# A state-space block with attention and routed experts on one core: three input blocks per half, the residual added on TensorE, ones brought in by transfers

## The reference

```python
x_in, z = split(x @ W_in)                         # 512 + 512 features
x_in = silu(sum(x_pad[:, k:k+L] * W_conv[k] for k in range(4)) + b_conv)
dbc = x_in @ W_xproj                              # 64 + 16 (B) + 16 (C)
dt = softplus(dbc[..., :64] @ W_dt + b_dt)
def step(state, inp):                             # state [batch, 512, 16], 512 steps one after another
    dA = exp(clip(dt_t[:, :, None] * A, -10, 10))
    state = clip(state * dA + x_t[:, :, None] * (dt_t[:, :, None] * B_t[:, None, :]), -10, 10)
    y_t = einsum('bdn,bn->bd', state, C_t) + D * x_t
y = y * silu(z)
out = y @ W_out                                   # added to what the attention and expert branch gives
```

## Time and profile before

| | |
|---|---|
| three runs | 4441.67 us median, 4422.38 to 4448.53 |
| profiled execution, own time | 4426.43 us |
| its span | 4424.3 us |
| busy: PE, PEld | 3743.7 us (85%), 2801.6 us (63%) |
| busy: DVE, ACT, POOL | 2973.9 us (67%), 2502.9 us (57%), 2202.6 us (50%) |
| state-space part | from 2175.6 us to the end |

### The profile page before, as it was taken

The page is one execution under the profiler, slowest core; times in us unless marked ns, Lnnn a source line. Parts: engine busy times, 40 slices in busy tenths (PEclk is TensorE's granted clock), DMA queues, the critical chain, the costliest instruction groups (busy, mean ns, idle before and its releaser), DMA issues.

```text
span 4424.3 us, 70363 instructions
## 1 busy us (share of the span) xinstructions
PE 3743.7 (85%) x22136; PEld 2801.6 (63%) x22136; DVE 2973.9 (67%) x5485; ACT 2502.9 (57%) x6473; POOL 2202.6 (50%) x1120
## 2 busy tenths in 40 slices
PE   4888888888888875999869888889898998988886
PEld 2344444444444434777658888878787887888776
DVE  4455455544545522222269999999999999999997
ACT  1443343434433431333378777788778787777773
POOL 2223333333333221000067777777777787777774
PEclk8899999999999987999989999999999999999998
DMA  3322232223322214666522222222222222222221
GB/s 91 95 77 83 84 100 79 78 88 98 91 87 80 79 54 128 212 209 211 150 87 92 76 87 78 80 88 86 78 89 87 75 92 76 87 81 77 87 82 36
DMA packets 285737, 419.86 MB, mean 95 GB/s; under 512 B 77397, under 2 KB 249814, under 8 KB 262808
## 3 DMA queue, kind: packets, MB, share of 16 engines
q1 hardware_dynamic: 273048, 381.12, 26.6%
q0 software_dynamic: 12288, 33.57, 2.2%
HBM read 330.63 MB, written 83.17 MB: 94 GB/s over the span
## 4 chain that ended last, share of the span: by engine, by line
POOL 22%; issue 10%; PE 9%; DVE 8%; ACT 1%; DVEq 0%; POOLq 0%; DMA 0%; SPq 0%; ACTq 0%
POOL m_ub L1530 18%; PE m_Y L1884 7%; DVE m_PR L1734 2%; DVE m_S L1742 2%; DVE m_PR L1742 2%; DVE m_S L1734 1%; POOL m_th_z L1515 1%; POOL m_yg L1540 1%; DVE m_ub L1719 1%; ACT m_dA L1640 1%; POOL m_dtx L1509 1%; PE m_F L1846 1%; PE m_F L1895 0%; PE m_F L1820 0%; DVEq L1733 0%
## 5 line engine op out<-in xcount | busy, mean ns | idle before, releaser
L1530 POOL TENSOR_TENSOR m_ub<-m_Bb,m_dtx 128x2048 f32<-128x2048 f32 x256 | 1157.7, 4546 | 440.4 <-PE m_Y L1884 434.0
L1640 ACT ACTIVATE m_dA<-m_dt,m_a_neg 128x128 f32<-128x128 f32 x4096 | 1211.0, 387 | 168.8 <-DVE m_S L1742 167.6
L1884 PE MATMUL m_Y<-m_ub,m_ident 128*128 128x128 f32 x8192 | 1040.4, 293 | 204.6 <-DVE m_ub L1719 204.6
L1884 PEld LDWEIGHTS m_Y<-m_ub,m_ident 128*128 128x128 f32 x8192 | 1022.1, 208 | 218.4 <-DVE m_ub L1719 218.4
L539 ACT ACTIVATE f_pt<-f_X 128x512 f32<-128x512 f32 (+1 forms) x704 | 371.8, 554 | 712.9 <-PE f_X L841 691.2
L615 DVE TENSOR_REDUCE f_nm<-f_Y 128x1 f32<-128x512 f32 (+3 forms) x896 | 434.1, 530 | 354.4 <-PE f_Y L841 351.4
L1734 DVE SCALAR_TENSOR_TENSOR m_PR<-m_dA,m_S 128x512 f32<-128x512 f32 x512 | 355.6, 695 | 124.5 <-POOL m_ub L1530 53.8
L1734 DVE SCALAR_TENSOR_TENSOR m_S<-m_dA,m_PR 128x512 f32<-128x512 f32 x512 | 354.9, 693 | 12.0
L1742 DVE CUSTOM_DVE_ANT_1 m_PR<-m_PR,m_ub 128x512 f32<-128x512 f32 x512 | 353.2, 690 | 0.2 <-DVE m_PR L1734 0.2
L1742 DVE CUSTOM_DVE_ANT_1 m_S<-m_S,m_ub 128x512 f32<-128x512 f32 x512 | 353.2, 690 | 0.0
L1719 DVE TENSOR_TENSOR m_ub<-m_S,m_Cb 128x512 f32<-128x512 f32 x512 | 349.7, 683 | 0.0
(11 more groups left out here) (229 smaller groups left out, 6278.4 us busy)
## 6 DMA issues: line engine op xcount, KB each, us to landing
m_Bb<-m_bc_dram SPq DMA_DIRECT2D x64, 1024.0 KB, 4.6
m_Cb<-m_bc_dram SPq DMA_DIRECT2D x64, 1024.0 KB, 4.7
f_parts_dram<-f_parts SPq DMA_DIRECT2D x32, 768.0 KB, 4.1
f_kst<-f_parts_dram SPq DMA_DIRECT2D x192, 128.0 KB, 2.6
f_qst<-f_parts_dram SPq DMA_DIRECT2D x192, 128.0 KB, 2.6
e_rows<-sorted_rows SPq DMA_DIRECT2D x70, 256.0 KB, 2.7
e_wg<-Wg SPq DMA_DIRECT2D x70, 256.0 KB, 2.9
e_wu<-Wu SPq DMA_DIRECT2D x70, 256.0 KB, 3.9
```

The source lines that it names most:

```text
L1530: pool.tensor_tensor(ub[:, h, i, :, :], Bb[:, s, :, :], dtx[:, par, m, None, s * SN:(s + 1) * SN].to_broadcast([P, NST, SN]), ALU.mult).th ...
L1640: last = act.activation(dA[:, h, i, n, :], dtt[:, par, m, s * SN:(s + 1) * SN], ACT.Exp, scale=a_neg[:, m, n:n + 1])
L1884: last = pe.matmul(Y[:, i * SN:(i + 1) * SN], ident[:, :], ub[:, h, i, n, :], start=False, stop=(n == NST - 1), skip_group_check=True)
```

## The change

In the state-space part `ub` gets a third block per half. Inputs go to blocks 0 and 1; `times_c` writes to blocks 1 and 2, and `nsum` reads those. So the inputs of block 0 need only the end of the scan of unit u-2, and those of block 1 only the first half of its `nsum`. Room for it comes from tiles that now share storage: `xn` is `xm`, `sp_u` is `th_z`, `sp_v` is `th_x`, `ot` is `res`, and `dtx` is single. Waits go with that: the load of rows waits for the transposes, the load of `res` for the store of the chunk before, and the two tanh of ScalarE for the dt of the chunk before. `add_res` goes away: TensorE adds `res` with two more matmuls of 128x256 at the end of `project_out`, and ScalarE copies F[2] out (`copy_out`). For the very first unit, dt, dt times x and the inputs are made on VectorE instead of GpSimd.

In the attention part the two memsets of ones go away; ScalarE issues six transfers of one partition each from a tile of ones, and the waits of ScalarE and TensorE for all weights move to "T" and "lat" of the first sequence.

```diff
-        fixed(pool.memset(onesb)) among the later constants      # now among the first seven
-        act.wait_ge(w_loaded, W_ALL)
+        act.wait_ge(const_ready, N_CONST_FIRST)
+        for p in range(2):
+            for q in range(PARTS):
+                act.dma_start(kst[p][KS + q:KS + q + 1, :, :]..., onesb[:, 0:NH * SEQ // P]).then_inc(q_scaled, 16)
...
-        for p in range(2):
-            dve.memset(kst[p][KS:KS + PARTS, :, :], 1.0).then_inc(q_scaled, 1)
...
-    xn = sb("m_xn", [P, TT, DM])
+    xn = xm
-    sp_u = sb("m_sp_u", [P, MI, CN])
-    sp_v = sb("m_sp_v", [P, MI, CN])
+    sp_u = th_z
+    sp_v = th_x
-    dtx = sb("m_dtx", [P, 2, MI, CN])
+    dtx = sb("m_dtx", [P, MI, CN])
-    ub = sb("m_ub", [P, 2, 2, NST, SN])
+    ub = sb("m_ub", [P, 2, 3, NST, SN])
-    ot = sb("m_ot", [P, TT, DM])
+    ot = res
...
         def load_res(c):
-            held(ot_done, c)
+            held(ot_stored, 16 * c)
...
         def inputs_of(c, par, u):
-                    pool.wait_ge(nsum_done[pu], 2 * (pc - 1) + i + 1)
+                    if i == 0:
+                        pool.wait_ge(s_step, NU * ST * (pc - 1) + ST * (pu + 1) + 2)
+                    else:
+                        pool.wait_ge(nsum_done[pu], 2 * (pc - 1) + 1)
...
+        def copy_out(c):
+            act.wait_ge(outp_done, c + 1)
+            act.wait_ge(ot_stored, 16 * c)
+            act.activation(ot[:, :, :], F[2][:, :, :], ACT.Copy).then_inc(ot_done, 1)
...
             if not first:
                 decays(c, par, 2)
+                copy_out(c - 1)
             if not last:
                 softplus(c + 1)
...
-            return dve.tensor_tensor(ub[:, h, :, :, cols], ...        # times_c
+            return dve.tensor_tensor(ub[:, h, 1:3, :, cols], ...
-                                in1=ub[:, h, :, :, cols]...           # scan
+                                in1=ub[:, h, 0:2, :, cols]...
...
+        dve.tensor_tensor(sp_u[:, :, :], sp_u[:, :, :], sp_r[:, :, :], ALU.add).then_inc(sp_sub, 1)
+        dve.tensor_tensor(dtt[:, 0, :, :], sp_u[:, :, :], sp_v[:, :, :], ALU.subtract).then_inc(dt_ready, 1)
+        dve.tensor_tensor(dtx[:, :, :], x2[:, 0, :, :], dtt[:, 0, :, :], ALU.mult).then_inc(dtx_ready, 1)
+        for i in range(2):
+            dve.tensor_tensor(ub[:, 0, i, :, :], Bb[:, 0, :, :], dtx[:, i, None, 0:SN]..., ALU.mult).then_inc(u_ready[0], 1)
...
-                slots[1][1] = lambda: add_res(c - 1)
...
-                    last = pe.matmul(Y[:, ...], ident[:, :], ub[:, h, i, n, :], ...)
+                    last = pe.matmul(Y[:, ...], ident[:, :], ub[:, h, 1 + i, n, :], ...)
...
+            pe.wait_ge(res_loaded, 16 * (c + 1))                      # project_out
+                last = pe.matmul(F[2][:, j, :], ident[:, :], res[:, j, :], start=False, stop=True)
```

More of the change, by code:

```diff
@@ L564, in do @@
             if kind == "T":
+                if isinstance(b, int) and b == 0:
+                    act.wait_ge(w_loaded, W_ALL)
                 for k in range(KM):
@@ L784, in project @@
             if kind == "lat":
+                if isinstance(b, int) and b == 0:
+                    pe.wait_ge(w_loaded, W_ALL)
                 pe.wait_ge(*used(("T", 0), r))
@@ L1690, in body, with tail @@
                 decays(c + 1, 1 - par, 1)
-        chunk_order(body, lambda c, par: None)(nc.scalar)
+        def tail(c, par):
+            copy_out(c)
+        chunk_order(body, tail)(nc.scalar)
     @block.vector
@@ L1755, in gate_y @@
                               zs[:, par, 2 * h:2 * h + 2, s * SN:(s + 1) * SN], ALU.mult).then_inc(yz_done, 1)
-        def add_res(c):
-            dve.wait_ge(outp_done, c + 1)
-            dve.wait_ge(res_loaded, 16 * (c + 1))
-            dve.wait_ge(ot_stored, 16 * c)
-            dve.tensor_tensor(ot[:, :, :], F[2][:, :, :], res[:, :, :], ALU.add).then_inc(ot_done, 1)
         dve.wait_ge(ident_ready, 4)
@@ L1799, in tail @@
             gate_y(c, par, NU - 1)
-            add_res(c)
         chunk_order(body, tail)(nc.vector)
@@ L1883, in nsum @@
                 for n in range(NST):
-                    last = pe.matmul(Y[:, i * SN:(i + 1) * SN], ident[:, :], ub[:, h, i, n, :], start=False, stop=(n == NST - 1),
+                    last = pe.matmul(Y[:, i * SN:(i + 1) * SN], ident[:, :], ub[:, h, 1 + i, n, :], start=False, stop=(n == NST - 1),
                                      skip_group_check=True)
@@ L1897, in project_out @@
                 for k in range(TOPK):
-                    last = pe.matmul(F[2][:, j, :], wdiag[:, k, j, :], yg[:, k, j, :],
-                                     start=False, stop=(k == TOPK - 1))
+                    pe.matmul(F[2][:, j, :], wdiag[:, k, j, :], yg[:, k, j, :], start=False, stop=False)
+                last = pe.matmul(F[2][:, j, :], ident[:, :], res[:, j, :], start=False, stop=True)
             last.then_inc(outp_done, 1)
```

37 lines of the change are left out of this document (23 added, 14 removed).

## The result

The changed kernel takes 4374.28 us (median of 4 runs, 4365.18 to 4385.42). In the same session the kernel before took 4443.73 (4 runs), 69.5 more. The recorded ratio of the two is 0.9864, with an interval of 0.9833 to 0.9894; it is not the plain quotient of these medians, which is 0.9844. The forecast was 4355 with a range of 4330 to 4395.

What follows compares the result with a forecast made beforehand. VectorE, 95% busy, was taken to pace the loop. Gains of 48.3 + 14.7 + 6.3 + 7.0 - 0.4 = 75.9 us against 4426.43 gave 4350.5; 4.5 added for a low-lying execution made 4355 us, range 4330 to 4395.

Steps and rivals of the forecast that it cites:

- chunk 1's wait: VectorE's wait at u0 of chunk 1, 3.9 us, taken out of the loop's gain and counted with the start.
- the end: At the end of the program ScalarE's copy and TensorE's added matmuls lie open: 0.4 us more.
- Part 1: Third block of `ub` in the scan loop: the wait for `nsum` goes at every unit; gain 48.3 us.
- the stop in `gather`: GpSimd's stop of 5.68 us inside `gather`, which nothing releases; 4.8 us of VectorE's wait behind it stays.
- rival (a): GpSimd's row is the bound, the wait returns at u0: 4371 if 1 us too long, 4387 if two; chance 0.09.
- Part 2: `add_res` moved to TensorE and ScalarE: 0.48 us per chunk off VectorE, gain 14.7 us, copy hidden by `log_rest`.
- Part 3: First unit's inputs on VectorE: 2.4 us stays at the start, 6.3 us in all with the next `nsum` wait gone.
- issue: VectorE's 13 loop waits of 2.3 us each, taken as the branch back, which the change leaves.
- Part 4: Start of attention: the reciprocal comes near 16.3 us instead of 23.33; gain 7.0 us, bounds 5 and 8.
- (b): VectorE's loop waits of 0.5 to 1 us aren't due to `nsum`: only 20.2 us gained, near 4411; chance 0.04.
- (c): Attention gains nothing at its start, as the ones' transfers or the weights come late: 4362; chance 0.06.
- (d): ScalarE's late copy closes a ring through TensorE: slower from near 5.7 us late, 4500 at 8 us; chance 0.03.

Runs made afterwards that it cites:

- two_blocks_add: The changed kernel with two blocks of `ub` again and the residual added by VectorE again: 4433.04 us, ratio 1.0013.
- add_res_back: The changed kernel, three blocks kept, with the residual added on VectorE again, without the added matmuls and ScalarE's copy: 4390.40 us, ratio 0.9907.
- copies4: The changed kernel with ScalarE's copy of F[2] done five times instead of once in each chunk: 4473.24 us, ratio 1.0080.

## Why the prediction came out as it did

The time lies in the range, 19 us above the forecast. The mechanism was right, and several sizes were off. Median to median the gain is 69.5 us for the 75.9 of the sum; that this is so near is in part the spread, as the profiles show 55.5 in the state-space part and 4.8 at the start. Taken apart along two_blocks_add and add_res_back, the part's 55.5 us are these (length of the part, forecast and measured):

| term | forecast | measured |
|---|---|---|
| three blocks, with chunk 1's wait | 48.3 + 3.9 = 52.2 less | 2260.4 - 2204.6 = 55.8 less |
| the residual, with the end | 14.7 - 0.4 = 14.3 less | 2204.6 - 2193.2 = 11.4 less |
| first unit on VectorE | 2.4 less | 2260.4 - 2248.7 = 11.7 more |
| sum | 68.9 less | 55.5 less |

Each measured term is the difference of two single executions, good to a few us. The shared tiles and their waits are in the row of the first unit.

**Part 1** was right by its own steps: block 0 ahead of TensorE, the waits gone, the stop in `gather` kept. It says which bound comes next, and there it was half right: GpSimd's row had 1.13 us instead of 0.8, so rival (a) stayed out, but ScalarE's row, through the convolution to `gate_y`, had 0.38 (2.0 in the second chunk of a body). Both are margins, so neither row held VectorE up in this kernel.

**Part 2** was right in the loop, 0.92 us a body for 0.96; the 11.4 over the part for 14.3 isn't told from the spread. That the copy costs nothing held, but not only `log_rest` stands behind it: with 0.38 us less to spare it would have held up `gate_y`. Its worth depends on part 1, which the sum took as independent. Without the third block the same edit loses 24.3 us.

**Part 3** is the term that was wrong: 14 us off, and 9.8 of it are the 13 second stops. The prediction said that "issue" is the branch back "and the change leaves it". The change didn't touch the branch, but it put instructions ahead of the loop and so moved the loop's code (by 7 in all against the kernel before: 9 more from part 3, 2 fewer by the memsets of part 4). Of the start no gain was left at the first branch back. The remaining 2 us of the 14 are within the spread.

**Part 4** had the right place and the wrong landing: 4.8 us for 7.0, just below its lower bound of 5. The six more transfers of small pieces were allowed 1 us, and the weights came 3 us later with them.

For the profiled execution the sum gave 4350.5 us, and it took 4385.42. Of these 34.9 us, 13.4 are the part's length, and 21.5 lie around it: 2.2 for part 4, and the rest the spread between executions, which one profile of each kernel can't tell from a gain.

Of the rivals, (a) and (b) didn't occur (49 waits of GpSimd for TensorE in the loop, 169.0 us, against 67 and 315.5, and none that reached VectorE). The prediction's figure for (b) is wrong by its own terms: 14.7 + 6.3 + 7.0 - 0.4 - 3.9 is 23.7, not 20.2, so near 4407. (c) was wrong, as the start did gain. (d) didn't occur. copies4 shows where a late copy costs: it held TensorE at F[2] by at most 0.7 us, and the loss came by ScalarE's decays and the convolution, from a delay of 0.4 us on, not 3.3.
